# Attention and mixture-of-experts layer on one core: expert pair tables made in the first stage, the last batch weighed into four banks, and a new order between the two stages

## What is computed

```python
xn = layernorm(x)
s  = softmax(causal((xn @ WQ) @ (xn @ WK).T / 16)) @ (xn @ WV)
scores = softmax(xn @ w_gate.T)            # 8 experts, in 4 groups of 2; expert_bias added for the choice
topk_idx, weights                          # the 2 best groups, and in them the 2 best experts of each token
flat_idx = topk_idx.reshape(-1)
routed_in = xf[flat_idx] * weights         # flat_idx holds EXPERT numbers, 0 to 7: only the first 8 tokens are ever read
h = silu(grouped_mm(routed_in, w1, counts)) * grouped_mm(routed_in, w3, counts)
out = (silu(xf @ sw1.T) * (xf @ sw3.T) @ sw2.T).at[flat_idx].add(grouped_mm(h, w2, counts))
result = x + s * silu(out)
```

## Time and profile before

| | |
|---|---|
| median of 3 runs | 237.82 us (237.39 to 237.92) |
| the profiled execution | 238.74 us |
| its span in the trace | 236.7 us |
| PE busy | 228.2 us, 96% of the span |
| DVE, ACT, POOL busy | 75%, 61%, 23% |

### The profile page before, as it was taken

One profiled execution on the slowest core, in us unless ns is written; L12 is line 12 of the kernel. 1 busy time (PEld: TensorE's weight loads), 2 busy tenths in 40 slices (PEclk: granted clock), 3 DMA queues, 4 the chain that ended last, 5 costly groups with the idle time before them and its releaser, 6 DMA issues.

```text
span 236.7 us, 4676 instructions
## 1 busy us (share of the span) xinstructions
PE 228.2 (96%) x1533; PEld 205.6 (87%) x1533; DVE 176.6 (75%) x620; ACT 144.9 (61%) x392; POOL 55.3 (23%) x107
## 2 busy tenths in 40 slices
PE   7899999999999999999999999999999999999983
PEld 5688898998999989989899998898988889898843
DVE  3878669788797888877777875668676867859665
ACT  2454755756557556485575542878778696778722
POOL 5220732706318055091012000002020210202000
PEclk9999999999999999999999979999999999999999
DMA  6599430110200200000000000115847547383522
GB/s 198 186 318 307 150 91 1 29 59 6 89 3 1 88 3 3 0 0 3 0 0 4 0 3 0 48 38 187 178 86 183 91 132 129 100 204 63 131 78 100
DMA packets 18758, 19.45 MB, mean 82 GB/s; under 512 B 1064, under 2 KB 17712, under 8 KB 18736
## 3 DMA queue, kind: packets, MB, share of 16 engines
q1 hardware_dynamic: 15568, 16.02, 21.3%
q0 software_dynamic: 3168, 3.15, 8.8%
HBM read 14.95 MB, written 4.21 MB: 81 GB/s over the span
## 4 chain that ended last, share of the span: by engine, by line
PE 92%; DVE 2%; DMA 1%; ACT 1%; POOL 1%; issue 1%; DVEq 0%; ACTq 0%
PE bank L392 85%; PE bank L484 4%; PE bank L440 3%; DMA x_ring<-in_L_attn_x 1%; DVE raw_sw L1381 1%; POOL rstd L333 1%; DVE w L1379 1%; PE bank L556 1%; PE bank L414 0%; DVE bn L1088 0%; DVE arena L949 0%; ACT xT_hi_all L731 0%; ACT arena L731 0%; ACT probs L731 0%; ACT attn_all L731 0%
## 5 line engine op out<-in xcount | busy, mean ns | idle before, releaser
L392 PE MATMUL bank<-xT_hi_all,arena 128*128 128x512 f32 (+3 forms) x256 | 79.5, 367 | 0.7 <-DVE arena L949 0.7
L392 PE MATMUL bank<-arena 128*128 128x256 f32 (+2 forms) x560 | 76.8, 285 | 0.3 <-ACT attn_all L731 0.3
L392 PEld LDWEIGHTS bank<-arena 128*128 128x128 f32 (+1 forms) x560 | 72.0, 186 | 4.9 <-issue 0.8
L392 PEld LDWEIGHTS bank<-xT_hi_all,arena 128*128 128x128 f32 x256 | 46.8, 189 | 6.8 <-DVE arena L949 0.9
L731 ACT ACTIVATE arena<-bank 128x512 fp32r<-128x512 f32 (+4 forms) x84 | 36.2, 453 | 26.8 <-PE bank L392 25.2
L949 DVE TENSOR_TENSOR arena<-bank,arena 128x264 fp32r<-128x264 f32 (+4 forms) x83 | 41.5, 509 | 15.0 <-ACT arena L731 14.7
L392 PE MATMUL bank<-xT_lo_all,arena 128*128 128x512 f32 (+3 forms) x128 | 45.8, 358 | 0.0
L383 POOL DMA_DIRECT2D x_ring<-in_L_attn_x x6 | 7.9, 1316 | 79.0 <-DVE x_ring L1317 79.0
L392 PEld LDWEIGHTS bank<-xT_lo_all,arena 128*128 128x128 f32 x128 | 24.2, 189 | 2.2
L731 ACT ACTIVATE attn_all<-bank,row_inv 128x256 f32<-128x256 f32 x32 | 15.2, 474 | 16.4 <-PE bank L392 15.6
L761 ACT ACTIVATE probs<-bank,neg_max 128x128 f32<-128x128 f32 (+3 forms) x32 | 17.0, 530 | 9.5 <-DVE neg_max L1007 9.4
(11 more groups left out here) (127 smaller groups left out, 368.3 us busy)
## 6 DMA issues: line engine op xcount, KB each, us to landing
x_ring<-in_L_attn_x SPq DMA_DIRECT2D x7, 512.0 KB, 3.5
x_ring<-in_L_attn_x POOLq DMA_DIRECT2D x6, 512.0 KB, 5.8
out<-x_ring SPq DMA_DIRECT2D x6, 512.0 KB, 3.3
spread<-pairs SPq DMA_DIRECT2D x14, 128.0 KB, 3.1
w_sb<-in_L_ffn_w SPq DMA_DIRECT2D x1, 1024.0 KB, 10.9
raw_sw<-in_L_ffn_sw SPq DMA_DIRECT2D x3, 256.0 KB, 4.5
x_ring<-in_L_attn_x SPq DMA_DIRECT2D x2, 256.0 KB, 2.9
xn<-in_L_attn_x SPq DMA_DIRECT2D x1, 512.0 KB, 5.5
```

What stands on the lines that cost most here:

```text
L392: return nc.tensor.matmul(dst, lhsT, rhs, start=start, stop=stop, skip_group_check=True, **kw)
```

## The change

The pair tables move into the first stage, in the steps of batches 2 to 5, two experts' weights of each kind at a time. ACT (`table_high`) and POOL (`table_low`) split the weights into fp32r parts (`w_split`), and PE (`tables(n)`, n = 0 to 3) has them as the moving operand: 8 matmuls of 256 columns with `first8` as stationary operand, 16 columns wide (8 high parts and 8 low parts of the tokens). The table comes out by rows, in two halves that have to be added. ACT copies it out (`table_keep`), SP writes it to a DRAM buffer and reads it back with the pair on the partition into `x_ring`, POOL adds the halves (`B_rows`, `A_sum`), and ACT and POOL make `A_stack` of it in the step of batch 6. The transpose of `A_T` and the `xn8` operation are gone.

The last batch's four `weigh` write into four banks and wait for no `keep_attn`. `hidden(0, ...)` and three of the `hidden(1, ...)` stand where the tables stood and in between. DVE has 12 of batch 6's 20 routing steps already in step 6. The end has one DVE operation more: B is multiplied before the transpose, and the result is copied.

```diff
+        A_stack = sb("A_stack", [P, P], F32R)
+        B_rows = sb("B_rows", [PAIRS, H])
+        first8 = sb("first8", [P, C, 16], F32R)
+        w_split = arena[:, 0:XT].rearrange("p (r h d) -> p r h d", r=2, h=2)
+        A_halves, B_halves = x_ring[:, 0, 0, :].rearrange("p (h d) -> p h d", h=2), x_ring[0:PAIRS, 0, 1, :].rearrange("p (h d) -> p h d", h=2)
+        tables_dram = nc.dram_tensor("tables", [2, E, 8, 2, H], F32).ap()
...
+        def table_weights(k):
+            return w13[:, k // 4, 2 * (k % 4):2 * (k % 4) + 2, :, :].rearrange("p e c h -> p (e c h)")
...
+            for b in range(1, TABLES + 1):
                 step(b)
+            for b in range(TABLES, LOOP1):
+                n, e4 = (b - TABLES) // 2, 4 * ((b - TABLES) % 2)
+                if b + 1 < LOOP1:
+                    step(b + 1)
+                sp.wait_ge(s["tables_kept"], b - TABLES + 1)
+                for h in range(2):
+                    sp.dma_start(tables_dram[n, e4:e4 + 4, :, h, :].rearrange("g j d -> j g d"),
+                                 table_cols[8 * h:8 * h + 8, :, :]).then_inc(s["tables_out"], 16)
+            sp.wait_ge(s["tables_out"], 16 * 8)
+            sp.wait_ge(s["xn_done"], B - 1)
+            for rows in (slice(0, PAIRS), slice(PAIRS, P)):
+                sp.dma_start(A_halves[rows, :, :], tables_dram[0, :, :, :, :].rearrange("g j h d -> (g j) h d")).then_inc(s["tables_back"], 16)
+            sp.dma_start(B_halves, tables_dram[1, :, :, :, :].rearrange("g j h d -> (g j) h d")).then_inc(s["tables_back"], 16)
...
+            pool.wait_ge(s["x0_lo"], C)
+            nc.gpsimd.tensor_copy(first8[:, :, 0:8], xT_hi_all[:, 0, :, 0:8]).then_inc(s["first8_ready"], 1)
+            nc.gpsimd.tensor_copy(first8[:, :, 8:16], xT_lo_all[:, 0, :, 0:8]).then_inc(s["first8_ready"], 1)
+            def table_low(k):
+                pool.wait_ge(s["table_hi"], k + 1)
+                nc.gpsimd.tensor_tensor(w_split[:, k % 2, 1, :], table_weights(k), w_split[:, k % 2, 0, :].bitcast(F32),
+                                        ALU.subtract).then_inc(s["table_lo"], 1)
...
+                if TABLES <= b + 1 < TABLES + 4:
+                    table_low(2 * (b + 1 - TABLES))
+                    table_low(2 * (b + 1 - TABLES) + 1)
...
+            pool.wait_ge(s["tables_back"], 16 * 3)
+            pool.wait_ge(s["scored"], 3 * (B - 1))
+            nc.gpsimd.tensor_tensor(B_rows[:, :], B_halves[:, 0, :], B_halves[:, 1, :], ALU.add
+                                    ).then_inc(s["b_ready"], 1)
+            pool.wait_ge(s["b_ready"], 1)
+            nc.gpsimd.tensor_tensor(A_sum[:, :], A_halves[:, 0, :], A_halves[:, 1, :], ALU.add).then_inc(s["a_summed"], 1)
+            pool.wait_ge(s["a_hi"], 1)
+            nc.gpsimd.tensor_tensor(A_stack[PAIRS:P, :], A_sum[PAIRS:P, :], A_stack[PAIRS:P, :].bitcast(F32), ALU.subtract
+                                    ).then_inc(s["a_ready"], 1)
+            pool.wait_ge(s["a_ready"], 1)
...
-                if i > 0 or b > 0:
+                if b == B - 1 and i > 0:
+                    pe.wait_ge(s["sw_ready"], i)
+                elif i > 0 or b > 0:
                     pe.wait_ge(s["attn_kept"], T * b + i)
-                split_products(pv_bank[:, 0:D], [(pT[:, i % 2, 0, j * P:(j + 1) * P], pT[:, i % 2, 1, j * P:(j + 1) * P],
+                dst = last_pv_banks[i] if b == B - 1 else pv_bank
...
+            def tables(n):
+                pe.wait_ge(s["first8_ready"], 2)
+                pe.wait_ge(s["v_lo"], T * (n + TABLES + 1))
+                for u in range(2):
+                    pe.wait_ge(s["table_lo"], 2 * n + u + 1)
+                    w = w_split[:, u, :, :].rearrange("p h (e c d) -> p h e c d", e=2, c=C)
+                    for c in range(C):
+                        for h in range(2):
+                            ins = mm(v_bank[0:16, u * D:(u + 1) * D], first8[:, c, :], w[:, h, :, c, :], c == 0 and h == 0, c == C - 1 and h == 1)
+                ins.then_inc(s["tables_summed"], 1)
...
+                if TABLES <= b < TABLES + 4:
+                    tables(b - TABLES)
...
-            def table(n, quarter):
-                pe.wait_ge(s["xn8_ready"], 1)
-                pe.wait_ge(s["sw_ready"], 1 + n)
-                for g in range(quarter * E // 4, (quarter + 1) * E // 4):
-                    for c in range(C):
-                        ins = mm(table_bank[n][:, g * 8:(g + 1) * 8], w13[:, n, g, c, :], xn8[:, c, :],
-                                 c == 0, c == C - 1)
-                ins.then_inc(s["tables_summed"], 1)
...
             turn_sw(2)
-            table(0, 0)
             weigh(b, 0)
             turn_probs(b, 2)
-            table(0, 1)
             weigh(b, 1)
+            pe.wait_ge(s["sw_ready"], 1)
+            pe.wait_ge(s["exp_done"], T * B - 1)
+            hidden(0, 0, 0, h1_bank, "h1_done")
             turn_probs(b, 3)
-            table(0, 2)
             weigh(b, 2)
-            table(0, 3)
+            pe.wait_ge(s["sw_ready"], 2)
+            hidden(0, 0, 1, h3_bank, "h3_done")
             weigh(b, 3)
...
-            pe.wait_ge(s["a_split"], 2)
-            nc.tensor.transpose(x_bank[0][:, 0:P], A_T[:, :].bitcast(F32), ident[:, :]).then_inc(s["a_turned"], 1)
-            table(1, 0)
-            pe.wait_ge(s["sw_ready"], 3)
-            pe.wait_ge(s["exp_done"], T * B)
-            hidden(0, 0, 0, h1_bank, "h1_done")
-            table(1, 1)
             pe.wait_ge(s["route"], ROUTED)
+            pe.wait_ge(s["attn_kept"], T * (B - 1) + 1)
             for n in range(4):
-                ins = mm(bc_bank[:, 0:P], ones_bf[:, :], at_least[:, :, :, :].rearrange("p t k e -> p (t k e)")[:, n * P:(n + 1) * P],
+                ins = mm(pv_bank[:, 0:P], ones_bf[:, :], at_least[:, :, :, :].rearrange("p t k e -> p (t k e)")[:, n * P:(n + 1) * P],
                          n == 0, n == 3)
             ins.then_inc(s["counted"], 1)
-            pe.wait_ge(s["pT_lo"], T * B)
-            hidden(0, 0, 1, h3_bank, "h3_done")
-            table(1, 2)
+            pe.wait_ge(s["exp_done"], T * B)
+            hidden(0, 1, 0, h1_bank, "h1_done")
+            hidden(0, 1, 1, h3_bank, "h3_done")
             pe.wait_ge(s["rows_ready"], 1)
+            pe.wait_ge(s["attn_kept"], T * B)
             turn_pairs()
             spread_pairs(0)
-            hidden(0, 1, 0, h1_bank, "h1_done")
+            hidden(1, 0, 0, h1_bank, "h1_done")
             pe.wait_ge(s["a_ready"], 1)
             gather(0, 0)
             spread_pairs(1)
+            hidden(1, 0, 1, h3_bank, "h3_done")
+            hidden(1, 1, 0, h1_bank, "h1_done")
+            gather(0, 1)
             pe.wait_ge(s["pairs_kept"], 1)
-            table(1, 3)
-            hidden(0, 1, 1, h3_bank, "h3_done")
-            gather(0, 1)
-            pe.wait_ge(s["attn_kept"], T * B)
-            pe.wait_ge(s["b_kept"], 1)
             mm(acc_bank[0:PAIRS, 0:2 * H], zero_bf[:, 0:PAIRS], zero_bf[:, 0:2 * H], True, True)
             def step2(i):
-                hidden(i, 0, 0, h1_bank, "h1_done")
-                hidden(i, 0, 1, h3_bank, "h3_done")
+                if i > 1:
+                    hidden(i, 0, 0, h1_bank, "h1_done")
+                    hidden(i, 0, 1, h3_bank, "h3_done")
                 shared_out(i - 1, 0)
                 accumulate(i - 1, 0)
                 gather(i, 0)
-                hidden(i, 1, 0, h1_bank, "h1_done")
+                if i > 1:
+                    hidden(i, 1, 0, h1_bank, "h1_done")
                 shared_out(i - 1, 1)
                 gather(i, 1)
                 hidden(i, 1, 1, h3_bank, "h3_done")
...
+            def table_high(n, u):
+                if n == 0 and u == 0:
+                    act.wait_ge(s["experts_loaded"], 16 * 6)
+                if n > 0:
+                    act.wait_ge(s["tables_summed"], n)
+                copy(w_split[:, u, 0, :], table_weights(2 * n + u)).then_inc(s["table_hi"], 1)
+            def table_keep(n):
+                act.wait_ge(s["tables_summed"], n + 1)
+                if n > 0:
+                    act.wait_ge(s["tables_out"], 16 * 2 * n)
+                copy(table_cols.rearrange("p e d -> p (e d)"), v_bank[0:16, :]).then_inc(s["tables_kept"], 1)
...
+                    table_keep(b - TABLES)
...
+                if b == B - 2:
+                    act.wait_ge(s["a_summed"], 1)
+                    copy(A_stack[:, :], A_sum[:, :]).then_inc(s["a_hi"], 1)
+                if TABLES <= b + 1 < TABLES + 4:
+                    table_high(b + 1 - TABLES, 0)
                 keep_attn(b, 2)
                 v_high(p, 3)
+                if TABLES <= b + 1 < TABLES + 4:
+                    table_high(b + 1 - TABLES, 1)
...
-            keep_attn(b, 0)
             p_high(b, 2)
             sw_high(2)
+            keep_attn(b, 0)
             p_high(b, 3)
             keep_attn(b, 1)
-            keep_attn(b, 2)
-            act.wait_ge(s["tables_summed"], 4)
```

(45 more changed lines are left out.)

154 lines of the change are left out of this document (86 added, 68 removed).

## The result

The changed kernel takes **235.02 us** (median of 4 runs, 234.90 to 235.39). Beside it the kernel before takes 237.79 (4 runs, 237.39 to 237.92): a ratio of 0.990, 95% interval 0.988 to 0.992, faster by 2.8 us. The forecast was 234.2, 3.6 less. The two profiled executions differ by 238.74 - 234.90 = 3.84.

A forecast was written before the change was run, and what follows sets the result against it. PE, holding 92% of the chain, was taken as the bound. Removing 8.8 us and adding 3.9, 1.0 and 0.3 gave 3.6 less: median 234.2 us, range 232.6 to 236.4.

The forecast's parts named there:

- The sum for the profiled execution: Whole kernel: 8.8 us removed, less 3.9, 1.0 and 0.3 added, 3.6 less; profiled 238.74 would become 235.1.
- the clock term: PE at half clock for 3.4 us from 137.56 to 140.96; 1.7 us saved if the clock stays up.
- The carry to the median: The profiled execution lay 0.9 above the median 237.82; PE's difference was taken to carry over, giving 234.2 us.
- The new table matmuls: PE, first stage: 32 fp32r matmuls of 256 columns at 0.122, one record each, 3.9 us added.
- F: Rival at the new table matmuls: two records each, 7.8 for 3.9, 238.1 us; chance 0.03.
- Steps 2 to 5 at no cost: First stage: added ACT, POOL and SP work costs PE nothing, covered by PE's work and the tables' 0.95 us.
- D: Rival in steps 2 to 5: POOL holds DVE, 0.5 us lost per step, 2.0 more, 236.2; chance 0.12.
- E: Rival in steps 2 to 5: two POOL subtractions each hold DVE 1.04 us; 4.5 more, 238.7; chance 0.05.
- The walk between the stages: Counting has 0.1 us to spare; shared_out(0, 0) waits 0.6, shared_out(0, 1) 0.3 to 0.4; 1.0 taken together.
- B: Rival between the stages: the new waits are absent as ACT and DVE overlap more; 233.2 us; chance 0.12.
- The gap and the banks: Before weigh(7, 2): the 0.50 us gap goes, as the last batch's weigh no longer waits for keep_attn.
- rival C: PE's clock falls again, at the two new waits or elsewhere: 1.7 us more, 235.9; chance 0.13.

The follow-up runs named there:

- experiment 1: The kernel before, run once more with no edit: median 237.66 us.
- experiment 5: The changed kernel, run again with no edit on another chip: 235.36 us.
- 7: The changed kernel with 16 of the 32 new table matmuls left out (only the high parts of the weights multiplied): 234.56 us.
- 6: The changed kernel with two more POOL subtractions in each of steps 2 to 5, into memory nothing reads: 237.78 us.
- 8: The changed kernel with 16 of the 32 table matmuls left out and row_max(b, 1) ahead of two route operations in DVE's queue: 233.84 us.
- 9: The changed kernel with four POOL subtractions per step 2 to 5 and row_max(b, 1) ahead of two route operations: 235.50 us.
- Experiment 4: The changed kernel with hidden(1, 1, 0) back behind the second gather, and h_high(0, 1), h_low(0, 1), one_hot(1, 0) earlier: 234.12 us.
- 2: The kernel before with a bank of its own for weigh(7, 2), all tables in place: 237.00 us.
- 3: The changed kernel with one bank for the last batch's weighs and ACT's copies back in their earlier places: 239.01 us.
- 10: The kernel before, still with one bank, with 16 of its 32 float32 table matmuls left out: 235.32 us.
- 11: The kernel before with 16 of its 32 table matmuls left out and weigh(7, 2) in a bank of its own: 234.81 us.

## Why the prediction was right, and where it was off

**The sum for the profiled execution: right.** It said 3.6 less than a trace whose clock had fallen; from the start the two traces differ by 220.56 - 216.94 = 3.6. Against the trace of before whose clock had not fallen the same sum without the clock term is 1.9, and measured are 218.94 - 216.9 = 2.0.

**The carry to the median: the step that failed.** "It lay 0.9 above the median of 237.82, and a difference in PE work carries over" took 3.6 from the median too. But 1.7 of the 3.6 were the half-speed stretch, which the earlier trace rows show for that execution and which a typical one does not have (experiment 1). That the profiled execution stood 0.9 above the median was the hint: its early start, 0.64 ahead of experiment 1's, hid part of the 1.7. By my own terms the median should have gone down by 1.9, to 235.9. It went down by 2.8, with four executions of each kernel, and by 2.4 in experiment 5. With all executions on record it is 2.2: the 65 of the kernel before without a fall have a median of 237.45, the 10 of the changed kernel one of 235.26. That is close to the 2.0 from the start, so some 0.6 of the 2.8 is the scatter of small samples, to which the start adds up to 0.9 us. The 234.2 was nearer to the result than its reasoning earned, and part of that nearness is luck.

**The new table matmuls**: forecast 3.9; the steps went from 15.25 to 16.16, so 4 x 0.91 = 3.6. One record each; F fell.

**Steps 2 to 5 at no cost: right, and thin.** PE has no idle time there. The cover that the forecast named, the tables' own 0.95 us ahead of `scores(b, 3)`, is what carried it: with half of those matmuls gone PE waits (7), and with one held operation more it waits too (6), so 0.20 us were to spare. D and E, the rivals built on POOL holding DVE, had the mechanism right, and E the size of the holds (1.05 and 0.9 us). They failed because the two don't add up: the first hold falls where DVE would stand idle for `scores(b, 1)` anyway (in 8 and 9, with that hold in place, DVE still waits 0.24 for PE ahead of `row_max(b, 1)`; in the kernel before it waits 0.76 for PE ahead of `row_max(b, 0)`). Only the second delays `row_max`, from 0.26 us ahead of the tables' start (8: 66.85 to 67.11) to 0.61 behind it, by 0.87 against a cover of 0.87 + 0.20.

The Trainium skill, "SBUF — State Buffer", section "Who interferes with whom", with its exclusive lock for a whole instruction, agrees with 1.27 and 1.12 us for 0.22 here, and better than the 0.39 for 0.19 of the earlier trace rows, which only showed the tail of one meeting.

**The walk between the stages: right.** It had 0.1 to spare at the counting (0.06), 0.6 before `shared_out(0, 0)` (0.67), and 0.3 to 0.4 before `(0, 1)` (0.28). B fell. Experiment 4 prices the two at 1.0 to 1.3.

**The gap and the banks**: the gap was worth 0.5 as forecast (2). What the forecast missed is that the banks are a condition of the rest: without them the new order loses 3.3 us (3), and the change would have made the kernel slower. That holds without the 0.66 of the counting too: 220.22 - 0.66 = 219.6 from the start, an estimate, against 218.94. Likewise half of the old tables bring 2.0 of 3.5 (10, 11). Work on PE that covers waits of others can't be priced by its duration alone, unless the same edit takes the waits away, as this one does.

**The clock**: rival C fell. With waits of up to 1.15 us between dense matmuls (3) the mean was 0.996 or more in all 12 executions. By the page "TensorE: Matmul & The Clock Gate" of the Trainium skill, section "HAM oscillation — how this bites in real kernels", waits between groups of matmuls throttle the engine each time. The waits in its example are more than twice the longest here, so the page does not say that waits like these do it, though the forecast let C follow from it; no run here has waits as long. Falls were seen only in the kernel before, with its gap and its 8-column tables together. With the gap taken away there was none in 12 executions (2), but at 13 falls in 78 chance alone would show that in one such dozen of nine (65/78 to the twelfth power is 0.11), so which of the two brings the fall was not settled. Nor do the 13 come evenly: 7 in the 41 executions of the kernel before that go with experiments 1 to 4, 6 in the 17 with 5 to 7, none in the 20 with 8 to 11.

**The end**: 0.3 forecast, 0.39 measured.

**Two slips of the working**, neither of which moves the forecast: the lower end of the range is 233.2 - 0.7 = 232.5, not 232.6, and the 0.19 of the earlier trace rows belongs to a reduction with one input; the operation of the earlier trace rows itself takes 0.19 too where POOL is at rest (L1070 at 139.06 us of that trace).

## What to carry to other kernels

Before a difference found in one profiled execution is taken off a median, ask of each term whether it is in the typical execution: a mean clock of 0.993 and a time 0.9 above the median say that one is not. Where PE work is removed, walk through the semaphores that it covered, one by one; and where work is added, ask what it now covers, since half of it removed brought 0.8 us of 1.8. When GpSimd reads and writes SBUF beside VectorE, put what others wait for (here `row_max`, with one input in PSUM) ahead of VectorE operations with two SBUF inputs: with that order two more GpSimd operations in each of four steps cost 0.2 to 0.3 us from the start, without it 2.5 to 2.6.

## What was not expected of the hardware

- A VectorE operation of 0.22 us with two SBUF inputs took 1.27 us when it met a GpSimd subtraction from its beginning, and 1.12, 1.09 and 0.95 in later meetings. Each further subtraction held one more of its kind: two in the changed kernel (65.84 and 67.09 are their ends, 65.74 and 67.00 those of the subtractions), three in experiment 6.
- A GpSimd subtraction of 512 columns took 1.26 us here, 1.04 where it normalises, and about 1.1 on 64 partitions.
- The same program ran its first `scores` 0.82 us apart in two executions (17.96 and 18.78), while its 30 opening matmuls took 4.84 us in the one and 6.16 in the other.
- Two matmuls of one group can hide a wait: 0.81 us for a pair that else takes 0.57, with no idle time shown.
